# Finishing the routed rows inside the expert tiles of a mixture of experts

## The chip, the cores and the metric

The kernel runs on one core of a Trainium2 chip. The metric is the device time of one execution in microseconds (us), the median of several runs. A core has a matrix engine (TensorE, PE; its weight loads are PEld), VectorE (DVE), ScalarE (ACT), GpSimd (POOL), a queue engine (SyncE, SP) and 16 DMA engines. SP, ACT and POOL issue DMAs from their own queues; POOL alone issues indirect ones, which gather or scatter rows by a list of row numbers.

## The reference

Two decoder layers with six sublayers, each followed by a residual add and a layer norm, on 32 x 100 = 3200 tokens of 256 numbers (float32). The change touches the last sublayer alone, a mixture of 32 experts of which each token uses one, beside one shared expert:

```python
x = hidden_states.reshape(-1, 256)                 # 3200 tokens
shared_out = (silu(x @ sg) * (x @ su)) @ sd        # 256 -> 512 -> 256
logits = x @ gate_w                                # 32 experts
e = argmax(logits, -1);  scores = sigmoid(max(logits, -1))
xs = x * scores[:, None]
routed_out[i] = (silu(xs[i] @ rg[e[i]]) * (xs[i] @ ru[e[i]])) @ rd[e[i]]
out = layernorm(x + shared_out + routed_out)       # no scale or shift
```

## The kernel before

`mixture_of_experts` runs last and has three blocks. All engines meet at a barrier where one block ends and the next begins (`Place.leave`). Within a block each engine runs its own list of instructions in the order written, and they wait for each other by counters (`Event`).

**`route_rows`** holds the 3200 tokens as 25 tiles of 128 rows in `me_acc`. It computes the logits, gives every token a row number in a list of slots ordered by expert (`me_slot_i`; each expert's part is filled up to whole tiles of 128 rows, at most `SLOTS` = 56 tiles), scales the tokens (`me_scaled`) and scatters them to the DRAM tensor `rows_in` by 25 indirect DMAs on POOL (L3482). Before that SP fills `rows_in` and the last 16 tiles of `rows_out` with zeros from `me_zeros` (L3462, L3465), and POOL waits for both. Meanwhile PE computes the shared expert, and VectorE adds its result, couple of tiles by couple, to `me_acc` (L3702); the last couples come at the very end of the block. SP loads the weights of the first four expert tiles (L3470, L3471).

**`expert_tiles`** goes over the first `FIRST` = 40 slot tiles (a second call for the remaining 16 stands behind a branch that is taken only when more than 40 are in use). For tile n, SP loads its rows (`ea_xe`, L3769) and its expert's weights (`me_we`, 1 MB, L3773, after the second matmul group of tile n-4; `me_wd`, 0.5 MB, L3775, after the last group of tile n-4); PE turns the rows, multiplies by gate, up and down weights; ACT copies and applies silu; VectorE multiplies (L3880) and copies the output from PSUM (`ea_ye`, L3886); ACT's queue stores it to `rows_out` (L3855). PE's order in one turn is gate of n+1, turn of n+2, up of n+1, down of n. There are four buffers (`DEEP`) of rows, weights and outputs and two of each PSUM bank.

**`collect_rows`** goes over the 25 token tiles in five groups of 5: POOL gathers the five tiles' routed rows back from `rows_out` by slot number (L3954), VectorE adds them to `me_acc` (L3994) and takes mean and variance (L3997, L4001), POOL normalises (L3964 to L3969), SP stores 640 KB to `out` (L3931).

The layer norm's POOL part for one tile is `norm_rows` (L144), which the earlier sublayers use and which the change calls too.

Of the kernel before, what the change touches and what calls it, by code (L numbers as in the profile page):

```python
# [18 lines left out]
F32 = mybir.dt.float32  # L19
# [3331 lines left out]
def mixture_of_experts(nc, x, gate, shared, experts, consts, rows_in, rows_out, out):  # L3351

    with ExitStack() as ctx:
        near = ctx.enter_context(nc.sbuf_tensor("me_acc", [P, TILES, D], F32))
        places = ctx.enter_context(nc.sbuf_tensor("me_slot_i", [P, TILES], I32))
        owners = ctx.enter_context(nc.sbuf_tensor("me_owner_i", [1, SLOTS], I32))
        far = ctx.enter_context(nc.sbuf_tensor("me_far", [1, 1], I32))
        with nc.sbuf_tensor("me_we", [P, DEEP, UP], F32) as we, nc.sbuf_tensor("me_wd", [P, DEEP, WIDE - UP], F32) as wd:
            route_rows(nc, x, gate, shared, experts, consts, rows_in, rows_out, near, places, owners, far, we, wd)
            more = nc.values_load(far[0:1, 0:1], min_val=0, max_val=1)  # L3360
            expert_tiles(nc, "ea", experts, rows_in, rows_out, owners, 0, FIRST, we, wd, True)
            with nc.If(more == 1):
                expert_tiles(nc, "eb", experts, rows_in, rows_out, owners, FIRST, SLOTS - FIRST, we, wd, False)
        collect_rows(nc, rows_out, near, places, out)

def route_rows(nc, x, gate, shared, experts, consts, rows_in, rows_out, acc, slot_i, owner_i, far, we, wd):
# [11 lines left out]
    with ExitStack() as ctx:  # L3379
# [7 lines left out]
        tile_no = cs[:, E + P + TILES:]  # L3387
# [47 lines left out]
        sent = a.sem("sent")  # L3435
        g_done = Event(a, "g_done", 1, 2)
# [16 lines left out]
        def _(sp):  # L3453
            for n in range(GROUPS):
                sp.dma_start(acc[:, n * T:(n + 1) * T, :], x_g[n]).then_inc(x_in[n], 16)
# [3 lines left out]
                if n == 1:  # L3459
# [3 lines left out]
                         mid_bcast(zeros[:, :], SLOTS * D // 1024)).then_inc(zeros_out, 16)  # L3463
            skipped = SLOTS - FIRST
            sp.dma_start(rows_out[FIRST * P:, :].rearrange("(p a) d -> p (a d)", p=P).rearrange("p (k b) -> p k b", b=1024),  # L3465
                         mid_bcast(zeros[:, :], skipped * D // 1024)).then_inc(zeros_out, 16)
# [110 lines left out]
        def _(act):  # L3577
# [9 lines left out]
            def scale_rows(n):  # L3587
                act.activation(scaled[:, n, :], acc[:, n, :], ACT.Copy, scale=gain[:, n:n + 1]).then_inc(scaled_done, 1)
# [23 lines left out]
        def _(dve):  # L3612
# [84 lines left out]
            def add_shared(d):  # L3697
# [3 lines left out]
                rows = acc[:, tiles[0]:tiles[-1] + 1, :]  # L3701
# [29 lines left out]
def expert_tiles(nc, tag, experts, rows_in, rows_out, owner_i, first, count, we, wd, loaded):  # L3731

    with ExitStack() as ctx:
# [6 lines left out]
        ye = a.sb("ye", [P, DEEP, D])  # L3740
# [9 lines left out]
        stored_y = [Event(a, f"stored_y{n}", 1, unit=16) for n in range(DEEP)]  # L3750
# [7 lines left out]
        ye_done = Event(a, "ye_done", 1, 2)  # L3758

        rows_in_t = rows_in.rearrange("(t p) d -> t p d", p=P)  # L3760
        rows_out_t = rows_out.rearrange("(t p) d -> t p d", p=P)
# [3 lines left out]
        def _(sp):  # L3765
            for n in range(count):
                s, i = n % DEEP, n // DEEP
                sp.wait_ge(*etr_done.at(n, 1 - DEEP))
                sp.dma_start(xe[:, s, :], rows_in_t[first + n]).then_inc(xe_in[s].sem, 16)  # L3769
                if i or not loaded:  # L3770
# [4 lines left out]
                    sp.dma_start(wd[:, s, :], experts[e][:, UP:]).then_inc(wd_in[s].sem, 16)  # L3775

        @block.gpsimd
        def _(pool):
            open_all(pool, *we_in, *wd_in, *xe_in, *stored_y)
            identity(pool, ident, setup, 0)  # L3780

        @block.tensor
        def _(pe):
# [31 lines left out]
            def down(n):  # L3815
# [3 lines left out]
                pe.wait_ge(*ye_done.at(n, -1))  # L3819
# [19 lines left out]
        def _(act):  # L3839
# [20 lines left out]
            for n in range(count):  # L3860
# [4 lines left out]
                if n >= 1:  # L3865
                    store_y(n - 1)
            store_y(count - 1)
            for s in range(DEEP):
                act.wait_ge(*stored_y[s].at(len(range(s, count, DEEP)), 0))

        @block.vector
        def _(dve):
            open_all(dve, h_done, ye_done)
# [8 lines left out]
            def copy_y(n):  # L3882
                s = n % DEEP
                dve.wait_ge(*stored_y[s].at(n // DEEP, 0))
                dve.wait_ge(*y_done.at(n, 1))
                dve.tensor_copy(ye[:, s, :], yo[n % 2][:, 0:D]).then_inc(ye_done.sem, 1)  # L3886

            times_up(0)
            for n in range(count):
                if n + 1 < count:  # L3890
                    times_up(n + 1)
                copy_y(n)

def collect_rows(nc, rows_out, acc, slot_i, out):

    T = 5
    GROUPS = TILES // T
    PAIRS = GROUPS // 2
    with ExitStack() as ctx:  # L3900
        a = Place(nc, ctx, "cr")
        half = a.sb("half", [P, T])
        index = a.sb("index", [P, 2, T], I32)
        yg = a.sb("yg", [P, 2, T, D])
        z = a.sb("z", [P, 2, T, D])
        stats = a.sb("stats", [P, 2, T, 6])
        mv = a.sb("mv", [P, 2, T, 2])
        rstd = a.sb("rstd", [P, 2, T])
        nbias = a.sb("nbias", [P, 2, T])
        xn = a.sb("xn", [P, 2, T, D])  # L3910
        turns = a.sem("turns")
        setup = a.sem("setup")
        got = [Event(a, f"got{n}", T, unit=16, one=0) for n in range(2)]
        index_done = Event(a, "index_done", 1)
        z_done = Event(a, "z_done", 1, 2)
        st_done = Event(a, "st_done", 1)
        mv_done = Event(a, "mv_done", 1)
        xn_done = Event(a, "xn_done", 1, 2)
        stored = [Event(a, f"stored{n}", 1, unit=16) for n in range(2)]
        pool_step = a.sem("pool_step")  # L3920
        out_g = out.rearrange("(g t p) d -> g p t d", p=P, t=T)
        block = ctx.enter_context(nc.Block())

        @block.sync  # L3924
        def _(sp):
            open_all(sp, *stored)

            def store(m, u):
                n = 2 * m + u
                stand(sp, turns, *xn_done.at(n, 1))  # L3930
                sp.dma_start(out_g[n], xn[:, u, :, :]).then_inc(stored[u].sem, 16)  # L3931

            for m in range(0, PAIRS):
                store(m, 0)
                store(m, 1)
            store(PAIRS, 0)
            sp.wait_ge(*stored[0].at(PAIRS + 1, 0))
            sp.wait_ge(*stored[1].at(PAIRS, 0))

        @block.gpsimd  # L3940
        def _(pool):
            open_all(pool, index_done, xn_done)
            pool.memset(half[:, :], -0.5).then_inc(setup, 1)
            pool.wait_ge(setup, 1)

            def fetch(m, u):
                n = 2 * m + u
                pool.wait_ge(*z_done.at(n, -1))
                if not is_first(m):
                    stand(pool, turns, *got[u].at(m, 0))  # L3950
                pool.tensor_copy(index[:, u, :], slot_i[:, bass.ds(n * T, T)]).then_inc(index_done.sem, 1)  # L3951
                stand(pool, turns, *index_done.at(n, 1))
                for t in range(T):
                    pool.indirect_dma_start(yg[:, u, t, :], None, rows_out,  # L3954
                                            bass.IndirectOffsetOnAxis(ap=index[:, u, t:t + 1], axis=0)).then_inc(got[u].sem, 16)

            def norm(m, u):
                n = 2 * m + u
                chain = Chain(pool, turns, pool_step, n, 4)
                pool.wait_ge(*stored[u].at(m, 0))  # L3960
                stand(pool, turns, *mv_done.at(n, 1))

                root, shift = rstd[:, u, :], nbias[:, u, :]
                chain.then(pool.tensor_scalar(root, mv[:, u, :, 1], LN_EPS, None, ALU.add))  # L3964
                chain.then(pool.tensor_tensor(root, root, half[:, :], ALU.pow))  # L3965
                chain.then(pool.tensor_tensor(shift, mv[:, u, :, 0], root, ALU.mult))  # L3966
                chain.then(pool.tensor_scalar(shift, shift, -1.0, None, ALU.mult))  # L3967
                for t in range(T):
                    ins = pool.tensor_scalar(xn[:, u, t, :], z[:, u, t, :], rstd[:, u, t:t + 1], nbias[:, u, t:t + 1],  # L3969
                                             ALU.mult, ALU.add)  # L3970
# [151 lines left out]
```

## Time and profile before

| | |
|---|---|
| time, median of 3 runs | 3460.66 us (3458.9 to 3466.82) |
| the profiled execution's own time | 3464.54 us |
| its span, first to last instruction | 3462.8 us |
| mean granted TensorE clock | 0.901 |
| PE busy | 2902.8 us (84%) |
| DVE / ACT / POOL busy | 2292.2 (66%) / 1989.7 (57%) / 1436.8 us (41%) |
| DMA | 185.52 MB, mean 54 GB/s |

The shares are means over seven stages with different limits. The mixture of experts is the last part: it begins near 3002 us of the span, its expert tiles near 3166, its collecting stage near 3395. The page's rows of tenths show these as the last six of 40 slices, with the DMA engines full in the middle and nearly only POOL in the last one.

### The profile page before, as it was taken

To read this page: it belongs to the slowest core of one execution; us is meant where nothing else is said; L and a number is where in the kernel's file an instruction comes from. 1 tells how busy PE (TensorE), PEld (TensorE's weight loads), DVE (VectorE), ACT (ScalarE), POOL (GpSimd) and SP (SyncE) were. 2 spreads that over 40 slices of the span, in tenths; PEclk is the share of its full clock that TensorE was granted. 3 is DMA by queue.
4 is the path that set the end of the run, shared out by engine and by line. 5 is a ranking of instruction groups with operands and counts; after the bars stand their busy time and mean duration, and the time that the engine had idled before them with its cause. 6 is when DMAs were issued, how large, how long until landed. Compare 5 with 4: busy or idle time off the path is not lost. (4 is left out here: it accounts for less than half of the span.)

```text
span 3462.8 us, 70536 instructions
## 1 busy us (share of the span) xinstructions
PE 2902.8 (84%) x23440; PEld 1874.3 (54%) x23440; DVE 2292.2 (66%) x9975; ACT 1989.7 (57%) x5876; POOL 1436.8 (41%) x2205
## 2 busy tenths in 40 slices
PE   8999997799999933699976888888888888699991
PEld 4555554566767722355543444454545444467991
DVE  2445445577777778466647999999999999341112
ACT  3333331477777720577746998988898988421110
POOL 0122222366665627476642444545444444220006
PEclk9999998899999976799977989888898988699996
DMA  2000000211111101110010000000000000342992
GB/s 74 14 22 17 18 12 16 65 43 46 49 44 46 35 32 46 38 30 27 29 51 14 17 19 23 19 23 19 23 19 23 19 22 10 118 164 98 334 335 89
DMA packets 106148, 185.52 MB, mean 54 GB/s; under 512 B 10862, under 2 KB 89070, under 8 KB 100526
## 3 DMA queue, kind: packets, MB, share of 16 engines
q1 hardware_dynamic: 97614, 169.07, 14.9%
q0 software_dynamic: 2400, 6.56, 0.6%
q10 hardware_dynamic: 5760, 5.25, 0.4%
q8 instruction: 193, 3.16, 0.4%
q14 instruction: 181, 1.48, 0.1%
HBM read 143.22 MB, written 37.62 MB: 52 GB/s over the span
## 5 line engine op out<-in xcount | busy, mean ns | idle before, releaser
L3099 DVE MAX8 sa_cand<-sa_s 128x8 f32<-128x45 f32 (+3 forms) x3328 | 399.7, 190 | 30.8 <-ACT sa_s L2945 30.8
L914 ACT ACTIVATE ca_p<-ca_sm,ca_nb 100x361 f32<-100x361 f32 x512 | 301.0, 589 | 173.8 <-DVE ca_nb L995 173.4
L729 POOL TENSOR_SCALAR ca_p<-ca_p,ca_rec 100x361 f32<-100x361 f32 x512 | 281.9, 571 | 250.7 <-DVE ca_rec L1009 250.6
L2704 POOL TENSOR_SCALAR sa_s<-sa_s,sa_unit,sa_nu 128x361 f32<-128x361 f32 (+1 forms) x416 | 261.5, 646 | 204.2 <-DVE sa_nu L3191 204.2
L523 DVE RECIPROCAL ta_rec<-ta_den 128x400 f32<-128x400 f32 x64 | 169.6, 2650 | 246.6 <-PE ta_den L384 246.6
L2828 PE MATMUL sa_tr<-sa_ident,sa_s 128*128 128x128 f32 (+3 forms) x1248 | 229.9, 304 | 112.4 <-ACT sa_pT L2979 98.2
L995 DVE CUSTOM_DVE_ANT_0 ca_sm<-ca_sc,ca_mb 100x361 f32<-100x361 f32 x512 | 250.0, 526 | 59.2 <-PE ca_sc L816 59.1
L2961 ACT ACTIVATE sa_spare_a<-sa_s,sa_nu 128x361 bf16<-128x361 f32 (+1 forms) x416 | 247.2, 595 | 56.6 <-DVE sa_nu L3193 56.5
L2694 POOL TENSOR_TENSOR sa_over<-sa_cand,sa_tc 128x280 f32<-128x280 f32 (+3 forms) x128 | 99.5, 778 | 400.9 <-DVE sa_tc L3118 263.2
L2828 PEld LDWEIGHTS sa_tr<-sa_ident,sa_s 128*128 128x128 f32 (+3 forms) x1248 | 164.8, 160 | 181.1 <-ACT sa_pT L2979 127.1
L2953 ACT ACTIVATE sa_s<-sa_s,sa_nt 128x361 f32<-128x361 f32 (+1 forms) x416 | 248.4, 608 | 22.5 <-DVE sa_nt L3152 22.4
L288 POOL TENSOR_SCALAR_AFFINE_SELECT ta_pT<-ta_pT 100x400 f32<-100x400 f32 x128 | 66.5, 543 | 453.1 <-ACT ta_pT L466 453.0
L2814 PE MATMUL sa_sc<-sa_kT,sa_qm 32*128 32x361 f32 (+3 forms) x768 | 228.4, 523 | 22.5 <-ACT sa_s L2945 21.7
L827 PE MATMUL ca_tr<-ca_ident,ca_p 100*128 100x100 f32 (+1 forms) x1536 | 207.1, 257 | 7.5 <-ACT ca_pT L923 5.6
L3161 DVE TENSOR_SCALAR_CACHE_REDUCE sa_spare_d<-sa_s 128x361 bf16<-128x361 f32 (+1 forms) x416 | 203.4, 518 | 0.6 <-ACT sa_s L2953 0.3
L827 PEld LDWEIGHTS ca_tr<-ca_ident,ca_p 100*128 100x128 f32 (+1 forms) x1536 | 168.9, 151 | 63.2 <-issue 29.5
L2793 PE MATMUL sa_yo<-sa_wv,sa_cTs 128*128 128x256 f32 (+1 forms) x384 | 155.1, 544 | 55.7 <-DVE sa_vm L3088 55.7
L2979 ACT ACTIVATE sa_pT<-sa_tr 128x512 f32<-128x512 f32 (+5 forms) x384 | 178.6, 500 | 37.9 <-PE sa_tr L2828 37.7
L2945 ACT ACTIVATE sa_s<-sa_sc 128x361 f32<-128x361 f32 (+1 forms) x416 | 182.1, 473 | 17.6 <-PE sa_sc L2814 15.4
L1518 POOL TENSOR_TENSOR na_rs<-na_rs,na_half 100x32 f32<-100x32 f32 x32 | 174.5, 5453 | 2.7
L2814 PEld LDWEIGHTS sa_sc<-sa_kT,sa_qm 32*128 32x128 f32 (+3 forms) x768 | 83.2, 184 | 158.3 <-ACT sa_s L2945 107.2
L1697 ACT ACTIVATE na_p<-na_sm,na_nb 100x100 f32<-100x100 f32 x512 | 151.0, 369 | 25.1 <-DVE na_nb L1754 23.8
(313 smaller groups left out, 7112.8 us busy)
## 6 DMA issues: line engine op xcount, KB each, us to landing
me_we<-m_experts SPq DMA_DIRECT2D x40, 1024.0 KB, 7.6
me_wd<-m_experts SPq DMA_DIRECT2D x40, 512.0 KB
ca_cTs<-cT SPq DMA_DIRECT2D x32, 361.0 KB
sa_cTs<-cT SPq DMA_DIRECT2D x32, 361.0 KB
rows_in<-me_zeros SPq DMA_DIRECT2D x1, 7168.0 KB
ea_xe<-rows_in SPq DMA_DIRECT2D x40, 128.0 KB
rows_out<-ea_ye ACTq DMA_DIRECT2D x40, 128.0 KB, 7.3
ca_ms<-mask SPq DMA_DIRECT2D x32, 141.0 KB
```

The costliest lines, as they stand in the source:

```text
L729: ins = pool.tensor_scalar(p[:, r, j, :], p[:, r, j, :], rec[:, r, j:j + 1], 1.0, ALU.mult, ALU.mult)
L827: mm = pe.transpose(tr[f % 2][0:kn, j * S:(j + 1) * S], p[:, r, j, k0:k0 + kn], ident[0:S, 0:S])
L914: act.activation(p[:, r, j, :], sm[:, r % 2, j, :], ACT.Exp, bias=nb[:, r % 2, j:j + 1], scale=-1.0, accum_out=den[:, r, j:j + 1]).then_in ...
L995: dve.tensor_tensor_reduce(sm[:, r % 2, j, :], sc[j][0:S, 0:S2], mb[:, u, :], -1 / 4, 3e38, ALU.add, ALU.min, nb[:, r % 2, j:j + 1]).then_ ...
L2704: pool.tensor_scalar(s[0:rows, u, i, :], s[0:rows, u, i, :], unit[0:rows, :], nu2[0:rows, i:i + 1], ALU.mult, ALU.add).then_inc(p_done.sem, 1)
L2814: mm = pe.matmul(bank[0:rows, 0:S2], qm[hr, u, P * i:P * i + rows], kT[hr, u, i // 7, :], start=True, stop=True)
L2828: mm = pe.transpose(tr[f % 2][0:kn, c0:c0 + rows], s[0:rows, u, i, k0:k0 + kn], ident[0:rows, 0:rows])
L2945: act.activation(s[0:rows, u, i, :], sc[pos % SC][0:rows, 0:S2], ACT.Copy).then_inc(z_in.sem, 1)
L2953: act.activation(s[0:rows, u, i, :], s[0:rows, u, i, :], ACT.Relu, bias=nt0[0:rows, i:i + 1], accum_out=total[0:rows, i:i + 1]).then_inc(r ...
L2961: ins = act.activation(spare_a[0:rows, i, :], s[0:rows, u, i, :], ACT.Relu, bias=nu1[0:rows, i:i + 1], accum_out=total[0:rows, i:i + 1])
L3099: ins = dve.max(cand[0:rows, i, q, :], s[0:rows, u, i, PART[q]:PART[q + 1]])
L3161: ins = dve.tensor_scalar(spare_d[0:rows, i, :], s[0:rows, u, i, :], u1[0:rows, i:i + 1] if step else 0.0, 0.0, ALU.is_gt, ALU.add, accum_ ...
```

## The change

The collecting stage is taken out. `rows_out` gives way to `rows_acc`, a DRAM tensor of 56 x 128 rows of 257 numbers, filled with zeros. `me_acc` gets a 257th column that holds the token's number minus 3200. When the shared expert's result has been added to a couple of tiles, POOL scatters these tiles of `me_acc` to their slots in `rows_acc`, 25 more indirect DMAs behind those to `rows_in`. In each expert tile SP also loads the slot tile of `rows_acc` (`ea_near`); VectorE makes the row numbers from its last column (`ea_place`; an empty slot gives 3200), adds the rest to the expert's output straight from PSUM, and takes mean and variance; POOL normalises and scatters the rows to `out` by token, with a bounds check that drops row number 3200. The copy to `ea_ye` and the store on ACT's queue are gone.

```diff
 def route_rows(nc, x, gate, shared, experts, consts, rows_in, rows_acc, acc, slot_i, owner_i, far, we, wd, acc_sent):
...
-        zeros = a.sb("zeros", [P, 1024])
+        zeros = a.sb("zeros", [P, 4 * (D + 1)])
...
         def _(sp):
...
-            sp.dma_start(rows_out[FIRST * P:, :].rearrange("(p a) d -> p (a d)", p=P).rearrange("p (k b) -> p k b", b=1024),
-                         mid_bcast(zeros[:, :], skipped * D // 1024)).then_inc(zeros_out, 16)
+            sp.dma_start(rows_acc.rearrange("(p a b) d -> p a (b d)", p=P, b=4),
+                         mid_bcast(zeros[:, :], SLOTS // 4)).then_inc(zeros_out, 16)
...
         def _(pool):
+            pool.wait_ge(w_in, 32)
+            pool.tensor_copy(acc[:, :, D], token).then_inc(token_done, 1)
             pool.wait_ge(slot_done, 1)
             pool.wait_ge(zeros_out, 32)
             for n in range(TILES):
                 pool.wait_ge(scaled_done, n + 1)
                 pool.indirect_dma_start(rows_in, bass.IndirectOffsetOnAxis(ap=slot_i[:, n:n + 1], axis=0),
                                         scaled[:, n, :], None).then_inc(sent, 16)
+            pool.wait_ge(token_done, 1)
+            for d in range(COUPLES):
+                pool.wait_ge(*acc_done.at(d, 1))
+                for n in couple(DOWNS[d]):
+                    pool.indirect_dma_start(rows_acc, bass.IndirectOffsetOnAxis(ap=slot_i[:, n:n + 1], axis=0),
+                                            acc[:, n, :], None).then_inc(acc_sent, 16)
             pool.wait_ge(sent, 16 * TILES)
...
 def expert_tiles(nc, tag, experts, rows_in, rows_acc, out, owner_i, first, count, we, wd, loaded, acc_sent):
...
         def _(sp):
+            def load_near(n):
+                sp.wait_ge(*z_done.at(n, 1 - DEEP))
+                sp.dma_start(near[:, n % DEEP, :], rows_acc_t[first + n]).then_inc(near_in[n % DEEP].sem, 16)
             for n in range(count):
                 s, i = n % DEEP, n // DEEP
                 sp.wait_ge(*etr_done.at(n, 1 - DEEP))
                 sp.dma_start(xe[:, s, :], rows_in_t[first + n]).then_inc(xe_in[s].sem, 16)
+                if n == DEEP - 1:
+                    sp.wait_ge(acc_sent, 16 * TILES)
+                    for early in range(DEEP):
+                        load_near(early)
                 if i or not loaded:
...
                     sp.dma_start(wd[:, s, :], experts[e][:, UP:]).then_inc(wd_in[s].sem, 16)
+                if i:
+                    load_near(n)
...
         def _(pool):
             identity(pool, ident, setup, 0)
+            pool.memset(half[:, :], -0.5).then_inc(setup, 1)
+            pool.wait_ge(setup, 3)
+            def finish(n):
+                s, u = n % DEEP, n % 2
+                chain = Chain(pool, turns, pool_step, n, NORM_STEPS)
+                if n >= DEEP:
+                    pool.wait_ge(*stored[s].at(n // DEEP, 0))
+                pool.wait_ge(*mv_done.at(n, 1))
+                norm_rows(pool, chain, z[:, u, :], mv[:, u, :], rstd[:, u, :], nbias[:, u, :], half[:, :],
+                          xn[:, s, :], xn_done.sem)
+                chain.end()
+                pool.wait_ge(*xn_done.at(n, 1))
+                pool.indirect_dma_start(out, bass.IndirectOffsetOnAxis(ap=place[:, s:s + 1], axis=0), xn[:, s, :], None,
+                                        bounds_check=ROWS - 1, oob_is_err=False).then_inc(stored[s].sem, 16)
+            for n in range(count):
+                finish(n)
+            for s in range(DEEP):
+                pool.wait_ge(*stored[s].at(len(range(s, count, DEEP)), 0))
...
             def down(n):
-                pe.wait_ge(*ye_done.at(n, -1))
+                pe.wait_ge(*z_done.at(n, -1))
...
         def _(act):
-            def store_y(n):
-                s = n % DEEP
-                act.wait_ge(*ye_done.at(n, 1))
-                act.dma_start(rows_out_t[first + n], ye[:, s, :]).then_inc(stored_y[s].sem, 16)
...
         def _(dve):
-            def copy_y(n):
-                s = n % DEEP
-                dve.wait_ge(*stored_y[s].at(n // DEEP, 0))
-                dve.wait_ge(*y_done.at(n, 1))
-                dve.tensor_copy(ye[:, s, :], yo[n % 2][:, 0:D]).then_inc(ye_done.sem, 1)
+            def output(n):
+                s, u = n % DEEP, n % 2
+                dve.wait_ge(*near_in[s].at(n // DEEP, 1))
+                if n >= DEEP:
+                    dve.wait_ge(*stored[s].at(n // DEEP, 0))
+                dve.tensor_scalar(place[:, s:s + 1], near[:, s, D:D + 1], float(ROWS), None, ALU.add)
+                dve.wait_ge(*xn_done.at(n, -1))
+                dve.wait_ge(*y_done.at(n, 1))
+                dve.tensor_tensor(z[:, u, :], yo[u][:, 0:D], near[:, s, 0:D], ALU.add).then_inc(z_done.sem, 1)
+                dve.wait_ge(*z_done.at(n, 1))
+                dve.bn_stats(stats[:, u, :], z[:, u, :]).then_inc(st_done.sem, 1)
+                dve.wait_ge(*st_done.at(n, 1))
+                dve.bn_aggr(mv[:, u, :], stats[:, u, :]).then_inc(mv_done.sem, 1)
...
-def collect_rows(nc, rows_out, acc, slot_i, out):
...
```

## Rows read from the trace of the kernel before

**Rows 1.** Windows: busy us (instructions) of each engine, then clock, DMA share, GB/s.

```profile
3200.00:3250.00 50.00, 50.00 (x383) 48.14 (x383) 10.02 (x18) 7.85 (x18) 0.00 (x0) 1.00 0.94 334
...
3350.00:3400.00 50.00, 41.63 (x307) 39.45 (x306) 9.23 (x17) 5.83 (x13) 3.21 (x5) 0.95 0.58 204
3400.00:3463.00 63.00, 0.00 (x0) 0.00 (x0) 18.34 (x55) 0.00 (x0) 49.86 (x71) 0.50 0.32 100
```

**Rows 2.** Timeline of one expert tile: start us, us, engine, line, operation.

```profile
3301.94 0.42 DVE L3886 COPY ea_ye<-ea_yo 128x256 f32<-128x256 f32 x1 [1.01 <-PE ea_yo L3821]
3302.00 0.33 SPq L3775 DMA_DIRECT2D me_wd<-m_experts  x1
...
3303.76 0.33 SPq L3773 DMA_DIRECT2D me_we<-m_experts  x1
...
3307.45 0.42 DVE L3886 COPY ea_ye<-ea_yo 128x256 f32<-128x256 f32 x1 [1.01 <-PE ea_yo L3821]
```

**Rows 3.** Timeline: one group's add, statistics and normalising at an idle time.

```profile
2987.28 0.41 DVE L3203 TENSOR_TENSOR sa_z<-sa_yo,sa_xb 100x256 f32<-100x256 f32 x1
...
2988.19 0.18 DVE L3207 BATCH_NORM_AGGREGATE sa_mv<-sa_stats 100x2 f32<-100x6 f32 x1
...
2988.53 0.22 POOL L145 TENSOR_SCALAR sa_rstd<-sa_mv 100x1 f32<-100x1 f32 x1 [11.68 <-DVE sa_mv L3207]
...
2990.11 0.56 POOL L149 TENSOR_SCALAR sa_xn<-sa_z,sa_rstd,sa_nbias 100x256 f32<-100x256 f32 x1
```

**Rows 4.** Costliest groups by line, after 3395 us (mean ns, idle before).

```profile
L3954 POOL DMA_INDIRECT cr_yg<-rows_out,cr_index x25 | 24.4, 978 | 7.8 <-issue 5.8 <-POOL cr_index L3951 1.7 <-DVE cr_mv L4001 0.3
```

**Rows 5.** Timeline: end of the routing stage, start of the expert tiles.

```profile
3160.19 0.69 DVE L3702 TENSOR_TENSOR me_acc<-me_acc,me_yo 128x512 f32<-128x512 f32 x1 [3.03 <-PE me_yo L3550]
3163.64 0.69 DVE L3702 TENSOR_TENSOR me_acc<-me_acc,me_yo 128x512 f32<-128x512 f32 x1 [2.77 <-PE me_yo L3550]
3165.81 3.19 SPq L3769 DMA_DIRECT2D ea_xe<-rows_in  x5
3166.84 0.20 POOL L136 MEMSET ea_ident<- 128x128 f32 x1 [54.45 <-issue]
```

**Rows 6.** Instructions on the DRAM tensor rows_in: ns min/median/max, and landing.

```profile
L3482 POOL DMA_INDIRECT rows_in<-me_scaled,me_slot_i x25: 956/958/1913, 3079.9 to 3111.4; - x25
...
DMA to landing us min/median/max: 2.4/5.8/7.0
```

**Rows 7.** Timeline: last expert tile and first instruction of the collecting stage.

```profile
3391.74 0.42 DVE L3886 COPY ea_ye<-ea_yo 128x256 f32<-128x256 f32 x1 [1.30 <-PE ea_yo L3821]
3395.32 0.10 POOL L3943 MEMSET cr_half<- 128x5 f32 x1 [227.82 <-POOLq L111]
```

**Rows 8.** Stores of the tile ea_ye: time to landing.

```profile
DMA to landing us min/median/max: 1.7/7.3/8.7
```

**Rows 9.** DMA queues, 3200 to 3350 us: packets, MB, share of 16 engines; issues.

```profile
q1 hardware_dynamic: 11813, 46.36, 87.0%
q10 hardware_dynamic: 3899, 3.55, 6.8%
...
me_we<-m_experts SPq DMA_DIRECT2D x27, 1024.0 KB, 7.7
```

**Rows 10.** DMA queue of POOL's scatters to rows_in, 3079 to 3125 us.

```profile
q0 software_dynamic: 1200, 3.28, 17.8%
```

**Rows 11.** Windows of 5 us: zero fill, then weights beside scatters.

```profile
3020.00:3025.00 5.00, 5.00 (x40) 4.38 (x39) 0.69 (x1) 1.79 (x3) 0.00 (x0) 1.00 1.03 422
...
3040.00:3045.00 5.00, 5.00 (x23) 3.03 (x22) 1.20 (x3) 0.98 (x2) 0.00 (x0) 1.00 0.21 84
...
3100.00:3105.00 5.00, 5.00 (x20) 3.47 (x19) 0.99 (x2) 0.28 (x1) 3.83 (x4) 1.00 1.01 417
```

**Rows 12.** Timeline: VectorE's add and a POOL operation beside it.

```profile
3436.44 1.49 DVE L3994 TENSOR_TENSOR cr_z<-me_acc,cr_yg 128x1280 f32<-128x1280 f32 x1 [9.00 <-DMA cr_yg<-rows_out,cr_index]
3436.63 1.41 POOL L3967 TENSOR_SCALAR cr_nbias<-cr_nbias 128x5 f32<-128x5 f32 x1
```

More of the change, by code:

```diff
@@ L3348, in up_w, with mixture_of_experts @@
     return w[:, (KD + k) * F:(KD + k + 1) * F]
-def mixture_of_experts(nc, x, gate, shared, experts, consts, rows_in, rows_out, out):
+def mixture_of_experts(nc, x, gate, shared, experts, consts, rows_in, rows_acc, out):
     with ExitStack() as ctx:
-        near = ctx.enter_context(nc.sbuf_tensor("me_acc", [P, TILES, D], F32))
+        a = Place(nc, ctx, "mo")
+        acc_sent = a.sem("acc_sent")
+        near = ctx.enter_context(nc.sbuf_tensor("me_acc", [P, TILES, D + 1], F32))
         places = ctx.enter_context(nc.sbuf_tensor("me_slot_i", [P, TILES], I32))
@@ L3358, in mixture_of_experts, with route_rows @@
         with nc.sbuf_tensor("me_we", [P, DEEP, UP], F32) as we, nc.sbuf_tensor("me_wd", [P, DEEP, WIDE - UP], F32) as wd:
[L3359 removed]
+            route_rows(nc, x, gate, shared, experts, consts, rows_in, rows_acc, near, places, owners, far, we, wd, acc_sent)
             more = nc.values_load(far[0:1, 0:1], min_val=0, max_val=1)
[L3361 removed]
+            expert_tiles(nc, "ea", experts, rows_in, rows_acc, out, owners, 0, FIRST, we, wd, True, acc_sent)
             with nc.If(more == 1):
[L3363 to L3367 removed]
+                expert_tiles(nc, "eb", experts, rows_in, rows_acc, out, owners, FIRST, SLOTS - FIRST, we, wd, False, acc_sent)
+def route_rows(nc, x, gate, shared, experts, consts, rows_in, rows_acc, acc, slot_i, owner_i, far, we, wd, acc_sent):
     CUT = TILES // 2
@@ L3587, in scale_rows @@
             def scale_rows(n):
-                act.activation(scaled[:, n, :], acc[:, n, :], ACT.Copy, scale=gain[:, n:n + 1]).then_inc(scaled_done, 1)
+                act.activation(scaled[:, n, :], acc[:, n, 0:D], ACT.Copy, scale=gain[:, n:n + 1]).then_inc(scaled_done, 1)
             def silu(s):
@@ L3700, in add_shared @@
                 dve.wait_ge(*y_done.at(d, 1))
-                rows = acc[:, tiles[0]:tiles[-1] + 1, :]
+                rows = acc[:, tiles[0]:tiles[-1] + 1, 0:D]
                 dve.tensor_tensor(rows, rows, yo[d % 2][:, 0:len(tiles) * D].rearrange("p (t d) -> p t d", d=D),
@@ L3728, in _, with expert_tiles @@
                 add_shared(d)
-def expert_tiles(nc, tag, experts, rows_in, rows_out, owner_i, first, count, we, wd, loaded):
+def expert_tiles(nc, tag, experts, rows_in, rows_acc, out, owner_i, first, count, we, wd, loaded, acc_sent):
     with ExitStack() as ctx:
@@ L3739, in expert_tiles @@
         hT = a.sb("hT", [P, 2, F])
-        ye = a.sb("ye", [P, DEEP, D])
+        near = a.sb("near", [P, DEEP, D + 1])
+        place = a.sb("place", [P, DEEP], I32)
+        half = a.sb("half", [P, 1])
+        z = a.sb("z", [P, 2, D])
+        stats = a.sb("stats", [P, 2, 6])
+        mv = a.sb("mv", [P, 2, 2])
+        rstd = a.sb("rstd", [P, 2, 1])
+        nbias = a.sb("nbias", [P, 2, 1])
+        xn = a.sb("xn", [P, DEEP, D])
         g = [a.psum(f"g{n}") for n in range(2)]
@@ L3749, in expert_tiles @@
         xe_in = [Event(a, f"xe_in{n}", 1, unit=16) for n in range(DEEP)]
-        stored_y = [Event(a, f"stored_y{n}", 1, unit=16) for n in range(DEEP)]
+        near_in = [Event(a, f"near_in{n}", 1, unit=16) for n in range(DEEP)]
+        stored = [Event(a, f"stored{n}", 1, unit=16, one=0) for n in range(DEEP)]
         etr_done = Event(a, "etr_done", 1, DEEP)
@@ L3864, in _ @@
                     copy_e(n + 2)
[L3865 to L3869, printed above, removed]
         @block.vector
         def _(dve):
-            open_all(dve, h_done, ye_done)
+            open_all(dve, h_done, z_done, st_done, mv_done)
             def times_up(n):
@@ L3891, in _ @@
                     times_up(n + 1)
-                copy_y(n)
-def collect_rows(nc, rows_out, acc, slot_i, out):
[L3897 to L3970, printed above, removed]
-                ins.then_inc(xn_done.sem, 1)
-                chain.end()
-            fetch(0, 0)
-            fetch(0, 1)
-            norm(0, 0)
-            fetch(1, 0)
-            norm(0, 1)
-            for m in range(1, PAIRS):
-                fetch(m, 1)
-                norm(m, 0)
-                fetch(m + 1, 0)
-                norm(m, 1)
-            norm(PAIRS, 0)
-        @block.vector
-        def _(dve):
-            open_all(dve, z_done, st_done, mv_done)
-            def output(m, u):
-                n = 2 * m + u
-                dve.wait_ge(*got[u].at(m, T))
-                stand(dve, turns, *xn_done.at(n, -1))
-                dve.tensor_tensor(z[:, u, :, :], acc[:, bass.ds(n * T, T), :], yg[:, u, :, :], ALU.add).then_inc(z_done.sem, 1)
-                dve.wait_ge(*z_done.at(n, 1))
-                for t in range(T):
-                    ins = dve.bn_stats(stats[:, u, t, :], z[:, u, t, :])
-                ins.then_inc(st_done.sem, 1)
-                stand(dve, turns, *st_done.at(n, 1))
-                for t in range(T):
-                    ins = dve.bn_aggr(mv[:, u, t, :], stats[:, u, t, :])
-                ins.then_inc(mv_done.sem, 1)
-            for m in range(0, PAIRS):
-                output(m, 0)
-                output(m, 1)
-            output(PAIRS, 0)
@@ L4010 @@
+                output(n)
 SUM_ERROR = 2.0 ** -17
@@ L4060, in build @@
         mixture_of_experts(nc, rows[4], t["m_gate"], t["m_shared"], t["m_experts"], t["m_consts"],
-                           dram("rows_in", (SLOTS * P, D)), dram("rows_out", (SLOTS * P, D)), t["out"])
+                           dram("rows_in", (SLOTS * P, D)), dram("rows_acc", (SLOTS * P, D + 1)), t["out"])
 def kernel(**inputs):
```

22 lines of the change are left out of this document (14 added, 8 removed).

## The prediction

> **What bounds the kernel now.** I read the granted clock and the slices of the page first, then the table of windows over the last 500 us, then the timelines at both ends of the expert tiles, then the DMA queues. The stages before the mixture of experts are untouched, so only this last part matters. In the windows the expert tiles show PE busy for 50.00 of 50 us at full granted clock with the DMA engines at 0.94; the last 63 us show PE at 0, POOL busy 49.86 and DMA at 0.32 [rows 1]. So there are two limits: PE sets the pace of the 40 expert tiles, and POOL sets that of the collecting stage, in which nothing else of size runs. The period of a tile is the distance of two copies of its output, 3307.45 - 3301.94 = 5.51 us [rows 2]. The collecting stage is paid in series: the copy of the last tile starts at 3391.74 and the span ends at 3462.8, which leaves 71.1 us behind the last tile [rows 7]. Of these, 25 indirect DMAs alone hold POOL for 24.4 us and 7.8 us of gaps [rows 4].
>
> **What is removed.** All of those 71.1 us but a new tail. The copy of a tile (0.42 us of VectorE) and the store on ACT's queue go too; both are hidden.
>
> **The new tail.** After the last tile's matmul there is one chain for one tile: add, statistics, aggregate, four small POOL operations, normalise. The sparse stage has the same chain at an idle moment: add at 2987.28, normalise ends at 2990.11 + 0.56 = 2990.67, so 3.4 us [rows 3]. Then POOL waits for its own result and issues the scatter: a gap of 7.8/25 = 0.3 us [rows 4]. A scatter lands 2.4 us after its start on quiet DMA engines, 7.0 at worst [rows 6]; the engines are quiet by then, so I take 2.4. Closing a block: between the end of the last copy (3392.16) and the collecting stage's first instruction (3395.32) lie 3.16 us [rows 7], of which a store takes at least 1.7 to land [rows 8], so some 1.4 us. I count it twice, for the expert block with the branch behind it and for the outer place and the end of the program: 2.8 us (bounds 1.4 and, with all of the 3.16 counted each time, 6.3). Tail: 3.4 + 0.3 + 2.4 + 2.8 = 8.9 us. Gain: 71.1 - 8.9 = 62.2 us.
>
> **What is added to the routing stage.** The 25 further scatters (`acc` to `rows_acc`) stand on POOL's queue behind the 25 to `rows_in`. Those start at 3079.9 and the last at 3111.4, at 0.96 + 0.3 = 1.26 us each [rows 4, 6]. POOL then sits idle for 54.45 us before the expert tiles [rows 5], and 25 more need 31.5 us, so all but the last are hidden under the shared expert's matmuls. Not hidden are the two tiles of the last add: it ends at 3163.64 + 0.69 = 3164.33 [rows 5], and POOL then needs 2 x (0.3 + 0.96) = 2.5 us before it can reach the barrier at which VectorE already stands. The expert tiles start 2.5 us late. Below: 0, if the barrier had slack on POOL; above: 2 x (0.3 + 1.91) = 4.4, by the longest of the 25 [rows 6]. I take 2.5. The SP wait for these scatters stands behind four `xe` loads; the last scatter starts near 3165.9 and lands at 3168.3 (at 7.0 us, 3172.9), while SP's fourth load is issued about 3170.5, the old 3165.81 plus three quarters of 3.19 plus 2.5 [rows 5]. Queued behind this wait are `xe` and weights of tile 4, which wait for the first tile's matmuls anyway: nothing.
>
> The zero fill grows from 2.1 to 7.37 MB (56 x 128 rows of 1028 bytes). The old one runs at 422 GB/s and ends near 3041 [rows 11]; 5.27 MB more are 12.5 us, to 3054. What waits for it is POOL's first scatter at 3079.9 [rows 6], so 26 us cover it; at half the rate it would end near 3071, still covered.
>
> **What is added to each tile.** On VectorE: statistics, aggregate and the index, some 0.8 us net, beside 10.02 us busy in 50 [rows 1]: hidden under 5.51. On SP one more load, `near`, which waits for the add of four tiles before: the next `xe` and weights are issued up to 1 us later. Today weights are issued 3303.76 - 3301.94 = 1.8 us after a copy and land in 7.7 [rows 2, 9]; by the order of PE's program the matmuls that need them start three periods (16.5 us) after that copy, so 7.0 us are to spare, then 6.0. On POOL: 0.2 us from the aggregate, 2.1 us for the five operations [rows 3], 0.3 + 0.96 for the scatter: 3.6 us of 5.51, and 4.5 with the longest scatter [rows 6]. Hidden; two buffers of `z` leave it two periods.
>
> One row warns: a POOL operation of 5 columns took 1.41 us while VectorE's add of two SBUF tiles ran beside it, and ended with that add [rows 12]. If the multiplication (0.69 us) and the add (0.42) held POOL up so in every tile, it would stand at 4.7 us, and with the longest scatter each time at 5.6, just above the period: +0.1 x 39 = 4 us. The Trainium skill, page "SBUF — State Buffer", section "Who interferes with whom", says that VectorE holds the port shared with GpSimd when both its inputs are in SBUF, and not with one input there. The row agrees; here the added operations read PSUM or have one input, so by that rule nothing is added. My sum goes without those 4 us; they stay in the range.
>
> The DMA engines are the tight place. Weights and `xe` take 87.0% of the 16 engines, the stores 6.8% [rows 9]. The store goes (-6.8). The `near` load is the size of an `xe`: 1.66 MB a tile cost 87.0, so 131,584 bytes cost 6.9. The scatter writes 3200 rows over 40 tiles, 62.5% of a full one; a full one costs 17.8% x 46 us / 25 = 0.33 us [rows 10], so 0.2 us, 3.7%. Sum 94 - 6.8 + 6.9 + 3.7 = 97.8%: below the pace of PE. At twice the price for the 1028-byte rows of `near`, 104.7%, or 5.77 us: 36 loaded tiles x 0.26 = 9.4 us late, less the 6.0 to spare, +3.4 us. With the scatter doubled as well, 108.4%, +10.6 us.
>
> **Sum.** -62.2 + 2.5 = -59.7 us. The profiled execution took 3464.54 (span 3462.8); that gives 3404.8. The median of the runs is 3460.66, lower by 3.9, so my forecast for it is 3401.0.
>
> **Rivals.**
> *The DMA engines take over the pace.* For it: 97.8% is near full. Against it: 417 GB/s were moved in a full stretch of weights beside POOL's scatters [rows 11], and a tile will ask for 1.92 MB / 5.51 us = 348. Time: 3401 + 3.4 to 10.6, 3404 to 3412. Chance 0.10. The Trainium skill, "DMA: Bandwidth & Descriptors", section "Specifications", puts the HBM limit of a core at about 358 GB/s, which would leave 3% instead of 17%; the 417 of the row speaks against it here.
>
> *POOL takes over the pace, and the kernel is slower.* No scatter with a bounds check and dropped rows stands in this trace; if software handled every index at length, POOL's 3.6 us could pass 5.51, and then each of 39 tiles pays. The loss eats the gain at 5.51 + 59.7/39 = 7.04 us a tile, that is a scatter of 4.4 us where rows show 0.96 and at most 1.91 [rows 6]. At 4.7 us: 3401 + 39 x 1.83 = 3472. Chance 0.04 for slower; 0.05 for a pace between 5.6 and 6.9 us, 3405 to 3455.
>
> *The scatters do not replace the stage cleanly:* the last scatter lands in 7.0 us and closing costs 6.3: +8.1, 3409. Chance 0.04.
>
> **How the numbers follow.** My case has 0.76: 3401, its own range 3397 (barrier slack 2.5, one closing 1.4) to 3406. No change within 0.2% (what a measurement of this kernel can tell, 7 us) needs a POOL pace by chance at 7 us: 0.01. Faster: 0.76 + 0.10 + 0.05 + 0.04 = 0.95; slower 0.04. The range 3396 to 3412 takes in my case, the DMA pace and the long tail, 0.90 together; a tenth of that I leave to terms that miss at their edges.
>
> **What would show it.** Right: no `cr_` lines; span end some 9 us after the last expert matmul; copies of `ea_yo` replaced by adds 5.5 us apart; first `xe` load near 3168.3; DMA share 0.97 to 1.0 with PE still at 50 of 50; DMA_INDIRECT on POOL near 1 us. Wrong: PE waiting for `me_we`, or VectorE's `ea_z` for POOL's `ea_xn`; scatters of 2 us and more; a first `xe` load well past 3170.

## The result and the profile after

The changed kernel takes 3411.67 us (median of 4 runs, 3409.47 to 3418.28); the kernel before took 3459.78 beside it (4 runs, 3455.82 to 3466.82). The ratio is 0.9858, 95% interval 0.9839 to 0.9877: 48.1 us faster, where 59.7 were forecast. The profiled execution took 3409.47, with a span of 3407.8.

The stages ahead of the mixture of experts have the same code and still differ from run to run: over all profiles of this study the last stage starts anywhere between 2989 and 3005 us. Its own times are therefore compared. It is cut at four marks in the timeline: POOL's first memset of `me_ident`; the end of the last add into `me_acc`; the first `ea_trx` matmul; the start of VectorE's operation on the last `ea_yo`. Between them lie routing, handover and expert tiles; behind the last mark, the tail.

| us | before | after | difference | forecast |
|---|---|---|---|---|
| stage starts at | 3002.21 | 2993.96 | | |
| routing and shared expert | 162.12 | 161.93 | -0.2 | 0 |
| handover to the expert tiles | 3.67 | 10.26 | +6.6 | +2.5 |
| 40 expert tiles | 223.74 | 223.69 | 0 | 0 |
| tail | 71.06 | 17.96 | -53.1 | -62.2 |
| sum | 460.59 | 413.84 | -46.8 | -59.7 |

So the collecting stage went as forecast, the tiles stayed as they were, and the 13 us that are missing lie at two places: 4.1 in the handover, 9.1 in the tail.

The windows of the changed kernel, core 0 (columns as in [rows 1]):

```profile
3200.00:3250.00 50.00, 50.00 (x381) 48.10 (x380) 16.07 (x45) 7.85 (x18) 26.41 (x55) 1.00 0.99 352
3350.00:3400.00 50.00, 39.74 (x297) 37.73 (x295) 14.32 (x42) 5.83 (x13) 26.15 (x54) 0.93 0.52 190
3400.00:3408.00 8.00, 0.00 (x0) 0.00 (x0) 0.00 (x0) 0.00 (x0) 0.00 (x0) 0.50 0.02 5
```

Against [rows 1], the first line shows PE at 50.00 of 50 as before, POOL from 0 to 26.41, VectorE from 10.02 to 16.07 and the DMA engines from 0.94 to 0.99. The last line stands where POOL was busy for 49.86 of 63 us: 8 us in which no engine computes and the DMA engines stand at 0.02. That is time for waits and jumps, and it is where to look.

The DMA queues of the changed kernel between 3200 and 3350 us, beside [rows 9]:

```profile
q1 hardware_dynamic: 15650, 49.84, 94.6%
q0 software_dynamic: 1296, 2.37, 4.2%
...
me_we<-m_experts SPq DMA_DIRECT2D x27, 1024.0 KB, 7.2
```

Weights, `xe` and `near` take 94.6% (forecast 87.0 + 6.9 = 93.9), the scatters 4.2% (3.7). The weights land in 7.2 us (7.7 before).

The handover in the timeline of the changed kernel:

```profile
3155.20 0.69 DVE L3712 TENSOR_TENSOR me_acc<-me_acc,me_yo 128x512 f32<-128x512 f32 x1 [2.76 <-PE me_yo L3560]
3156.17 0.95 POOL L3492 DMA_INDIRECT rows_acc<-me_acc,me_slot_i  x1 [1.23 <-DVE me_acc L3712]
3157.43 0.96 POOL L3492 DMA_INDIRECT rows_acc<-me_acc,me_slot_i  x1 [0.30 <-issue]
3163.99 1.76 SPq L3798 DMA_DIRECT2D ea_xe<-rows_in  x4
3165.10 0.20 POOL L136 MEMSET ea_ident<- 128x128 f32 x1 [6.71 <-issue]
```

The last add ends at 3155.89, and two scatters follow, as forecast: they end at 3158.39, 2.5 us later. But SP issues its first `xe` only at 3163.99, 5.6 us after POOL's last work. In [rows 5] the last add ends at 3164.33 and `xe` is issued at 3165.81, 1.48 us later. The new gap before it is 4.1 us too long.

The tail in the timeline of the changed kernel (VectorE's last two adds, and POOL):

```profile
3388.12 0.42 DVE L3935 TENSOR_TENSOR ea_z<-ea_yo,ea_near 128x256 f32<-128x256 f32 x1 [0.95 <-PE ea_yo L3876]
3389.39 0.25 POOL L145 TENSOR_SCALAR ea_rstd<-ea_mv 128x1 f32<-128x1 f32 x1 [1.24 <-DVE ea_mv L3939]
...
3389.84 0.43 DVE L3935 TENSOR_TENSOR ea_z<-ea_yo,ea_near 128x256 f32<-128x256 f32 x1 [0.57 <-PE ea_yo L3876]
...
3392.36 1.09 POOL L3829 DMA_INDIRECT out<-ea_xn,ea_place  x1 [0.81 <-POOL ea_xn L149]
3393.53 0.25 POOL L145 TENSOR_SCALAR ea_rstd<-ea_mv 128x1 f32<-128x1 f32 x1
...
3395.13 0.56 POOL L149 TENSOR_SCALAR ea_xn<-ea_z,ea_rstd,ea_nbias 128x256 f32<-128x256 f32 x1
3396.49 1.09 POOL L3829 DMA_INDIRECT out<-ea_xn,ea_place  x1 [0.81 <-POOL ea_xn L149]
```

The last two tiles come 1.72 us apart, not a period apart, while POOL needs 4.13 us for one (3396.49 - 3392.36). So the last tile stands behind its neighbour on POOL: its scatter starts 6.65 us after its add, where 3.7 were forecast. From there to the end of the span are another 11.3 us, where 5.2 were forecast. SP's waits in the same profile, 3130 to 3430 us (line waited for: us in total, times, longest), show one of 4.0 us at L111, the barrier at which a place is left; before, the two of them took 1.0 together:

```profile
SPq L3380 <- PEq L3380: 56.3, 1, 56.3
SPq L3744 <- PEq L3744: 29.7, 1, 29.7
SPq L111 <- PEq L111: 5.1, 3, 4.0
```

### The profile page after: what moved, and what is told of

Same layout as the page of the kernel before. It is cut to its first block and busy times, and to the rows that moved or that the text cites. A ratio compares the mean times of both kernels' runs of the same rounds, so it can differ in the third digit from the quotient of the medians.

```text
span 3407.8 us, 70871 instructions
## 1 busy us (share of the span) xinstructions
PE 2892.1 (85%) x23440; PEld 1868.3 (55%) x23440; DVE 2300.0 (67%) x10040; ACT 1990.0 (58%) x5876; POOL 1525.7 (45%) x2396
```

## The experiments

Each is an edit of the changed kernel. A kernel with a single execution is read by its stages, cut at the same marks as above, and not by its one time.

**The last scatters moved into the expert block.** Theory: the handover is long because POOL comes late to the barrier that closes the routing block. The four scatters of the last two adds are issued behind that barrier, where only the first `near` loads wait for them.

```
# routing block, POOL
-            for d in range(COUPLES):
+            for d in range(COUPLES - 2):
...
# expert_tiles, POOL, behind its setup
+            if loaded:
+                for t in range(20, 24):
+                    pool.indirect_dma_start(rows_acc, bass.IndirectOffsetOnAxis(ap=slot_i[:, t:t + 1], axis=0),
+                                            acc[:, t, :], None).then_inc(acc_sent, 16)
```

> The last four tiles of the shared expert's sum are scattered by POOL at the head of the expert block instead of at the end of the routing block; nothing is left out. Handover is the time from the end of VectorE's last add in the routing block to the first matmul of the expert tiles: 3.67 us before the change, 10.26 after it. Theory 1, closing a block waits on POOL for its scatters in flight: the last scatter then starts 7 us before the last add ends, so the handover falls to 4 to 5.5 us and the span by as much. Rival, the block simply has more to close (semaphores, an outer place): the handover stays near 10. Both expect the tile period at 5.52 us.

The timeline of this kernel:

```profile
3152.03 0.69 DVE L3712 TENSOR_TENSOR me_acc<-me_acc,me_yo 128x512 f32<-128x512 f32 x1 [2.76 <-PE me_yo L3560]
3154.21 1.76 SPq L3798 DMA_DIRECT2D ea_xe<-rows_in  x4
...
3156.40 0.98 POOL L3820 DMA_INDIRECT rows_acc<-me_acc,me_slot_i  x1 [0.37 <-POOL ea_half L3816]
```

`xe` is issued 1.49 us after the last add ends (3152.72), as before the change, and the handover is 3.58 us instead of 10.26. SP now waits 8.3 us for the scatters ahead of the first `near` loads; the tiles do not feel it (223.28 us). The stage falls from 413.84 to 406.32. All 6.6 us of the handover, then, come from POOL being last at the barrier.

**Without the second call of the expert tiles.** `more` is not 1 with this input, so the call is jumped over. This kernel leaves the second call out altogether.

```
-            with nc.If(more == 1):
-                expert_tiles(nc, "eb", experts, ..., FIRST, SLOTS - FIRST, we, wd, False, acc_sent)
```

> The branch and the second call for tiles 41 to 56 are left out (with this input it is not taken). Tail is the time from the start of the last tile's add to the end of the span: 17.96 us after the change, of which 5.4 us lie behind the point at which SP passes the expert block's barrier. Theory 1, the engines' jump over the skipped code costs a wait of 4.0 us at the outer place's barrier that the collecting stage used to hide: the tail falls to about 14. Rival, the closing itself costs this: the tail stays at 17 to 18.

SP's waits at L111 in this kernel:

```profile
SPq L111 <- PEq L111: 1.6, 3, 0.7
```

```profile
L110 ACTq COMPARE_BRANCH  x1: 45/45/45, 3403.2 to 3403.2; - x1
L110 PEldq COMPARE_BRANCH  x1: 4117/4117/4117, 3403.3 to 3403.3; - x1
```

PE's takes 4.12 us, the other four 0.05 to 0.07; without the second call none of the five is there. The kernel before has the same jump, at the head of its collecting stage, where PE has nothing else to do:

```profile
L3924 PEldq COMPARE_BRANCH  x1: 4190/4190/4190, 3395.1 to 3395.1; - x1
```

**Without the outer place.** The counter `acc_sent` is cleared by the expert block, and the outer place with its barrier goes.

```
-        a = Place(nc, ctx, "mo")
-        acc_sent = a.sem("acc_sent")
+        acc_sent = nc.alloc_semaphore("mo_acc_sent")
...
+        if loaded:
+            a.sems.append(acc_sent)
```

> The outer place and its closing barrier are taken out; its one semaphore is cleared with those of the first expert block; the branch stays. If the 4.0 us wait is the outer place's closing, the tail falls from 17.96 to about 13 or 14 us; if it is the jump over the skipped code, the engines still pay it before the program ends, and the tail stays within 1 us of 17.96.

The longest wait at L111 falls to 0.6 us here too, but the tail stays at 17.54 us: 0.4 less. One barrier costs next to nothing; the 4.0 us were only seen there, and move to the end of the program when it is taken away: PE's COMPARE_BRANCH stands there now, 4.02 us long from 3414.6.

**A second `near` load in every tile.** The rows are loaded once more into a buffer that nothing reads, 131,584 bytes a tile, to see whether the DMA engines at 0.99 are the limit.

```
+        again = a.sb("again", [P, DEEP, D + 1])
...
+                sp.dma_start(again[:, n % DEEP, :], rows_acc_t[first + n]).then_inc(again_in[n % DEEP], 16)
```

> Each slot tile of the scattered sum is loaded a second time into a buffer that nobody reads, 131,584 bytes more a tile. Theory 1, the DMA engines at a share of 0.99 are at their limit: the share cannot grow, weights come late, PE waits for them, and the 40 tiles take 5 to 12 us longer in all. Rival, the share read from the packets overstates what is used, and 374 GB/s can be carried: the tile period stays at 5.52 us and the span moves by less than 2 us apart from the stages before.

The window of 50 us at the same place of its tiles:

```profile
3210.00:3260.00 50.00, 50.00 (x383) 48.14 (x382) 16.37 (x47) 7.85 (x18) 26.19 (x54) 1.00 1.01 374
```

PE stays at 50.00 of 50 and the 40 tiles take 224.02 us (223.69). 374 GB/s go through where 352 went at a share of 0.99: the share says that some packet is under way on each engine nearly all the time, not that no more could be moved. The one execution took 3418.3, above the changed kernel's median, but its stage started 7.2 us later and took 1.6 us more, 1.1 of these in the routing stage.

**What holds POOL at the end of the block.** Two scatters explain 2.5 of the 6.6 us. The first candidates for the other 4.1 were the scatters themselves: that POOL's engine finishes them later than the profile shows, or that the barrier waits until they have landed. The rival: POOL needs this time at the end of a block whatever it did last. The next three kernels tell these apart. With the scatters moved away as above, one gives POOL a memset of 0.2 us behind the last add, of an identity matrix that is not used again:

```
+            pool.wait_ge(*acc_done.at(COUPLES - 1, 1))
+            pool.memset(ident[:, :], 0.0).then_inc(token_done, 1)
+            pool.wait_ge(token_done, 2)
```

> As with the last four tiles scattered in the expert block (handover 3.58 us there), but POOL also waits for the last add of the routing block and then runs a memset of 0.2 us, so that it is again the last engine at the block's end, with no scatter behind it. Theory 1, POOL is slow to close only behind a scatter: handover 4.0 to 4.5 us. Rival, POOL is slow to close a block whenever it comes last: 7 us or more.

Its timeline:

```profile
3150.74 0.69 DVE L3715 TENSOR_TENSOR me_acc<-me_acc,me_yo 128x512 f32<-128x512 f32 x1 [2.77 <-PE me_yo L3563]
3151.49 0.20 POOL L3495 MEMSET me_ident<- 128x128 f32 x1 [6.00 <-DVE me_acc L3715]
3157.14 1.76 SPq L3801 DMA_DIRECT2D ea_xe<-rows_in  x4
```

No scatter is behind the last add, and `xe` still comes 5.45 us after the memset's end (3151.69). The handover is 7.88 us.

Another keeps the changed kernel as it is and lets POOL wait until the scatters to `rows_acc` have landed:

```
             pool.wait_ge(sent, 16 * TILES)
+            pool.wait_ge(acc_sent, 16 * TILES)
```

> The changed kernel, in which POOL also waits at the end of the routing block until all 25 scatters of the sum have landed. Handover after the change: 10.26 us, and SP passes the barrier 5.2 us after the last scatter's start. Theory 1a, the closing waits for the landing itself: the added wait costs nothing, handover within 0.5 us of 10.26. Rival 1b, the closing takes some 4.3 us behind POOL's last instruction whatever has landed: the wait of some 1.5 to 2 us behind the scatter's end comes on top, handover about 12.

The handover grows from 10.26 to 12.17 us. Were the landing already waited for, it would have stayed. The 4 us come on top of whatever POOL waits for.

The last one moves the scatters away, and leaves POOL nothing behind the last add but the wait for it:

```
+            pool.wait_ge(*acc_done.at(COUPLES - 1, 1))
```

> As memset_late, without the memset: POOL only waits for the routing block's last add and goes straight to the block's end (handover 7.88 us with the memset, 3.58 without either). Theory 2a, POOL's way out of a block takes some 4 us from its last wait, whatever it did: handover 7.0 to 8.0. Rival 2b, the 4 us belong to the completion of an instruction on POOL: handover 3.6 to 4.5.

Its timeline:

```profile
3160.28 0.69 DVE L3713 TENSOR_TENSOR me_acc<-me_acc,me_yo 128x512 f32<-128x512 f32 x1 [2.76 <-PE me_yo L3561]
3166.41 1.76 SPq L3799 DMA_DIRECT2D ea_xe<-rows_in  x4
```

From the add's end (3160.97) to `xe` are 5.44 us, and the handover is 7.53, with no instruction of POOL in between. So POOL needs 5.44 - 1.49 = 4.0 us from its last wait or instruction until the others pass the barrier with it, and both readings with the scatters fall.

The view of one source line shows what fills this time: a sequencer instruction DRAIN on POOL at the end of the block. One line each of five blocks follows. They are the routing block before the change, in which POOL issues 25 indirect DMAs; the changed kernel's expert block, with 40; the expert block with the moved scatters (first experiment), 44; the routing block of this last kernel, 46; and the routing block that waits for the landing, 50:

```profile
L3379 POOLq DRAIN  x1: 2096/2096/2096, 3115.6 to 3115.6; - x1
L3744 POOLq DRAIN  x1: 3326/3326/3326, 3399.0 to 3399.0; - x1
L3744 POOLq DRAIN  x1: 3652/3652/3652, 3388.8 to 3388.8; - x1
L3380 POOLq DRAIN  x1: 3816/3816/3816, 3161.2 to 3161.2; - x1
L3380 POOLq DRAIN  x1: 4142/4142/4142, 3160.4 to 3160.4; - x1
```

The DRAIN takes 0.083 to 0.084 us for each indirect DMA that POOL issued in its block. Moving four scatters took 0.33 us from one (4.14 to 3.82) and gave 0.33 to the other (3.33 to 3.65). A memset in front of it changed nothing (3.82 us), nor did the landing: in the changed kernel, with 50 and no wait for it, the DRAIN (from 3156.1, 6.44 us) begins beside the last two scatters and ends 4.15 us after them. In the expert block of the kernel before, where POOL issues none, it ends 0.07 us after POOL's last operation. What POOL works at during its DRAIN is not shown.

**Timed: the moved scatters, and a shorter queue on POOL.** The first kernel is the one with the moved scatters. The second has this too, and takes half of each tile's chain from POOL: POOL adds epsilon and takes the root, VectorE computes the shift and normalises, one tile behind its add, and POOL scatters one tile behind its root.

```
# expert_tiles, VectorE, behind output(n), for tile n - 1
+                dve.wait_ge(*rs_done.at(n, 1))
+                dve.scalar_tensor_tensor(nbias[:, u, :], mv[:, u, 0:1], -1.0, rstd[:, u, :], ALU.mult, ALU.mult).then_inc(sh_done.sem, 1)
+                dve.wait_ge(*sh_done.at(n, 1))
+                dve.tensor_scalar(xn[:, s, :], z[:, u, :], rstd[:, u, :], nbias[:, u, :], ALU.mult, ALU.add).then_inc(xn_done.sem, 1)
...
# POOL, in place of finish(n)
+                root(n)
+                if n >= 1:
+                    scatter(n - 1)
```

> The last four tiles scattered in the expert block, timed. By its stage the span is 7 us shorter than that of the changed kernel (handover 3.58 against 10.26), so a median of 3403 to 3407 us against 3411.67; if the stages before hide or return it, 3409 to 3413.

> As late_timed, and POOL keeps only the root of the variance and the scatter; VectorE does the shift and the normalising, one tile behind. The forecast left out that the last two tiles come 1.7 us apart and queue on POOL, 4.1 us each. If that queue is on the path, the tail falls from 18 us to 15.5 to 16.5 and the median by 2 us below late_timed; if the closing alone sets the end, the tail stays at 18. If VectorE's longer turn delays the tiles, their period rises above 5.52 us.

| us | time, median (5 runs) | ratio to before, 95% | stage | tail |
|---|---|---|---|---|
| moved scatters | 3410.04 (3402.94 to 3415.42) | 0.9851 (0.9837 to 0.9864) | 408.53 | 18.07 |
| and the shorter queue | 3407.95 (3405.08 to 3409.49) | 0.9849 (0.9836 to 0.9862) | 405.22 | 15.29 |

The stage shows both steps: 413.84, 408.53, 405.22. The time of the whole does not show the first, since 12 us lie between the runs of one kernel. The tail gives back 2.8 us (18.07 to 15.29): the queue on POOL was on the path. VectorE's longer turn did not delay the tiles (223.87 us for 40). The last comparison was made for the sum of both steps, with the changed kernel unaltered on the same chip:

> The changed kernel itself, timed beside the next one on the same chip. Stage from the start of the mixture of experts to the end of the span: 413.8 us in its profile. Median 3407 to 3415 us.

> The version with late scatters and the work split, timed again beside the changed kernel. By its stage (405.2 us) it should be 8.6 us faster than that; if the earlier stages return the gain, the medians differ by less than 3 us.

The changed kernel took 3413.09 us (4 runs, 3407.89 to 3417.48; ratio to before 0.9858, 0.9837 to 0.9878), the edited one 3405.87 (5 runs, 3403.22 to 3408.99; 0.9839, 0.9823 to 0.9856): 7.2 us less. Their stages are 414.49 and 405.04, 9.5 us apart; the two intervals overlap, but the stage repeats within 0.7 us for either kernel (413.84 and 414.49; 405.22 and 405.04). The tail of the edited kernel:

```profile
3387.63 0.42 DVE L3945 TENSOR_TENSOR ea_z<-ea_yo,ea_near 128x256 f32<-128x256 f32 x1
...
3388.81 0.41 DVE L3956 TENSOR_SCALAR ea_xn<-ea_z,ea_rstd,ea_nbias 128x256 f32<-128x256 f32 x1
3389.42 0.25 POOL L3829 TENSOR_SCALAR ea_rstd<-ea_mv 128x1 f32<-128x1 f32 x1
3389.75 0.57 POOL L3830 TENSOR_TENSOR ea_rstd<-ea_rstd,ea_half 128x1 f32<-128x1 f32 x1
3390.35 0.16 DVE L3954 SCALAR_TENSOR_TENSOR ea_nbias<-ea_mv,ea_rstd 128x1 f32<-128x1 f32 x1 [1.13 <-POOL ea_rstd L3830]
3390.51 1.09 POOL L3836 DMA_INDIRECT out<-ea_xn,ea_place  x1 [0.19 <-issue]
...
3391.90 0.97 POOL L3836 DMA_INDIRECT out<-ea_xn,ea_place  x1 [0.30 <-issue]
```

The last scatter starts 4.27 us after the last add instead of 6.65, and the gap before a scatter is 0.2 to 0.3 us: the 0.81 appear only where POOL waits for its own normalising.

## Why the prediction was right, and where it was not

The direction, the mechanism and the range held: a stage of 71 us is replaced by a short tail, and the tiles keep PE's pace. The median of 3411.67 lies within 3396 to 3412 by 0.3 us, and beyond the likeliest case's own 3397 to 3406. That it lies inside is in part luck: timed again, beside a kernel before that was 4.1 us slower too, the changed kernel took 3413.09, and the upper end was there for a slower DMA pace or a late landing, neither of which came. Step by step:

*Removed.* All 71.1 us, and the store and copy cost nothing: right.

*The tail was mis-sized: 8.9 forecast, 17.96 measured.* The chain and the gap (3.7) took 6.65. They were taken from one tile at an idle moment [rows 3]; here two tiles end 1.72 us apart and POOL does them one after the other. The kernel before shows the same: the copy ahead of the last one (3391.74, [rows 7]) starts 1.73 us before it:

```profile
3390.01 0.42 DVE L3886 COPY ea_ye<-ea_yo 128x256 f32<-128x256 f32 x1 [1.01 <-PE ea_yo L3821]
```

The edit that shortens this queue took back 2.5 to 2.8. From the scatter's start to the end, 5.2 became 11.3. The trace accounts for all of it: 2.3 us until POOL's wait for the landing is over (3398.8), 3.3 of DRAIN (from 3399.0), 4.1 of PE's jump (from 3403.3), and some 1.6 between and behind these for the barriers and the end. The landing was forecast at 2.4; the closing, at 2.8, left out the DRAIN and the jump. The jump is also shown by leaving it out; that POOL is the last at this barrier too is read from the trace alone. The forecast counted the branch at the price of a barrier, since [rows 7] showed 3.16 us for store, barrier and branch together. The jump did not show there because PE's 4.19 us ran beside the collecting stage, in which PE has nothing to do.

*The handover was mis-sized: 2.5 forecast, 6.6 measured.* The two scatters cost what the rows said. What failed is the step that POOL, done with them, is at the barrier: it gets there 4.0 us after its last wait or instruction, behind the DRAIN. In the kernel before POOL had been idle for 54.45 us [rows 5], so its DRAIN of 2.10 us at 3115.6 was hidden; none of the rows that were read shows it, though the trace holds it. And the change itself made it longer, since its 25 more scatters double the count. The upper bound, 4.4 by a longest scatter, bounded the wrong term. Given as a sign of error was "a first `xe` load well past 3170": it came at 3163.99, in a stage that started 8.25 us earlier, so at 3172.2 on the old scale.

*The zero fill and the other 23 scatters.* Hidden, as forecast: the fill ended near 3047, and the routing stage kept its length (161.93).

*The tiles.* VectorE's additions, `near` and POOL's work are hidden, as forecast. POOL takes 4.13 us a tile instead of 3.6: the scatter 1.09 instead of 0.96 (all 40 of them 1092 to 1100 ns), its gap 0.81 instead of 0.3. That is below 5.51, and two tiles in a row is the only place where it counts. The bounds check alone does not explain the 1.09: the last scatter of the kernel with the shorter queue has it too and took 0.97. The four small operations were not held up beside VectorE: the root took 0.57 throughout.

*The rivals.* The DMA engines did not take over the pace, though the share came out at 0.99 against 97.8% forecast (a tile's weights and rows are 1.70 MB and not 1.66, so the sum should have read 97.6); the tile with 131,584 bytes more shows that room was left. The Trainium skill, "DMA: Bandwidth & Descriptors", section "Specifications", gives a core about 358 GB/s of HBM, as its half of what two cores share. With this kernel on one core that was no ceiling: 374 GB/s went through in that window. POOL did not take over the pace. The third rival, a closing dearer than thought, with 3409 at a chance of 0.04, is the one that came about in kind: it had the right place, and a longer landing as one of its two reasons, which was not it.

## What to carry to other kernels

An engine that is last at a block's closing barrier brings its own way out of the block with it. For POOL here that was a DRAIN of 0.083 us for each indirect DMA that it had issued in the block: 4.0 us on top of 2.5 of work. Moving the work behind the barrier, where something later waits for it, gave all 6.6 back. Where such an engine was always early the cost is hidden, but it can be read: look up the sequencer's instructions at the end of the block, DRAIN and COMPARE_BRANCH, and ask of each what will still run beside it after the change. Price a tail by the last tiles as they really come, back to back on the engine that finishes them, and a skipped branch as a cost wherever nothing runs beside it.

## What the runs showed of the hardware that was not expected

- POOL's 4.0 us from a last wait to a passed barrier, with or without an instruction in between (5.44 and 5.45 us to the next `xe`, against 1.49 when POOL is early).
- A DRAIN of POOL at a block's end that follows the number of indirect DMAs issued in the block, not the last operation: 2.10 us for 25, 3.33 for 40, 3.65 for 44, 3.82 for 46, 4.14 for 50.
- A jump past a call that does not run cost 4.0 us (tail 17.96 with it, 13.94 without). It was PE that took 4.12 us for it; the other engines took 0.05 to 0.07.
- A share of 0.99 of the DMA engines at 352 GB/s left room: 374 GB/s went through with the tiles as long as before.
- A scatter to `out` started 0.81 us after POOL's own normalising, and 0.2 to 0.3 us after POOL's last operation where VectorE had normalised.
- The stages ahead, unchanged in code, ended up to 16 us apart between executions, more than twice the 7 us that the text took for measurable.
